# A vision tower on one core: the router's and the low-rank stage's first tiles moved among the attention values, with two reorderings of the attention scores

## Chip, cores and metric

The kernel runs on one core of one Trainium2 chip. The metric is the device time of one execution in microseconds (us). Before the change three runs gave 822.62, 823.07 and 823.40 us, median 823.07.

Names: TensorE is PE, its weight load PEld, VectorE DVE, ScalarE ACT, GpSimd POOL, SyncE SP.

## What is computed

A batch of 128 images goes through a patch tokenizer (9 window tokens and a class token per image, 256 channels), then two layers of attention and a mixture:

```
h = tokenizer(x)                                   # [128 images, 10 tokens, 256]
h = h + attention0(layernorm(h))                   # over the 10 tokens, 16 heads of 16 channels, two scores masked
h = h + experts(layernorm(h))                      # 8 experts, top 2 by router logits x @ router_w
h = h + attention1(layernorm(h))                   # causal, scores clipped to +-10
z = layernorm(h)                                   # low-rank stage
out = h + z @ base_W.T + base_b + shared(z) + sum_e gate_e(z) * (z @ A_e.T) @ B_e.T
                                                   # 6 experts of rank 16, top 2 of softmax(z @ router_W.T + b)
```

In both attentions each image attends over its own 10 tokens. All arithmetic is float32.

## The kernel before, in words

The 128 images are the partitions and a "tile" t (0 to 9, T = 10) is one token of all images: h is [128, 10 x 256]. Each engine's program is written out by hand in order, and semaphores alone join them, so an instruction queued behind a waiting one waits with it. `phase` (L280) is a barrier of all engines; one stands ahead of attention 0's softmax (1), one behind the experts (2), one ahead of the low-rank stage (3).

**Attention scores.** TensorE makes query, key and value of a tile (L1281), ScalarE copies them out (L1352). A score is an elementwise product of 256 channels, summed by 16. VectorE multiplies and sums some rows itself (L1448, L1454); GpSimd makes the other products (L1122, jobs in the order of `pool_jobs`) and VectorE sums them (L1460). In layer 0 two columns' products are summed by TensorE instead (L1250: 16 matmuls with the identity). In `pool_end` GpSimd does jobs 4 and 5, then waits for the last row's variance and raises it to -1/2 (`inverse_std`), then jobs 6 to 9.

**Softmax.** The ten rows are two halves, tiles 0 to 4 and 5 to 9. Layer 0 (L1502 to L1513): maximum and subtraction of half 0, of half 1 (VectorE), exp of each (ScalarE, L1400), `spread_values` (ScalarE, L1361), then for each half sum, reciprocal and two scalings (L1470). In layer 1 the exp is per row (L1372); half 0 is scaled after VectorE has summed row 7.

**Values** (L1301, L1222, L1514). For tiles 0, 2, 4, 6, 8 (layer 1: 0 to 4, 6, 8) GpSimd multiplies values by weights (L1155) and, over 5 keys, folds the upper half of the keys onto the lower (L1170); TensorE sums the keys by matmuls with the identity and so transposes (L1315). The other tiles are VectorE's: product (L1180), sum (L1521), a transposition on TensorE (L300). ScalarE copies the result (L1407), TensorE projects it and adds h (L1332, L1333), ScalarE writes h (L1366), VectorE takes its mean and variance (`add_o`, L1535). `add_o(4)` comes behind VectorE's tile 9 in its queue. TensorE's order is:

```
for t in range(T):
    turn_o(t)              # the sum of tile t
    if t: project_o(t - 1)
project_o(T - 1)
```

**Router** (L1587, L1693, L1788). Behind the values: ScalarE normalises the rows in groups of tiles 0 to 3, 4 to 7, 8 and 9 (`norm_rows`; group 0 at t = 7 of the values), TensorE transposes (L1593) over three banks, ScalarE copies (L1699), TensorE makes 8 logits a tile (L294), VectorE finds the top two (L1795 to L1801) and builds the routing tables. Then come 27 slots of experts (L1631, L1639).

**Low-rank stage** (L1947 to L2041), behind barrier 3: ScalarE normalises ten tiles, TensorE transposes over four banks and multiplies by `z_w`, 118 columns (two banks); VectorE copies them (L2011) and adds the base bias to h. Then VectorE adds the router bias, ScalarE takes one exp of all ten tiles (L1999), VectorE finds the top two and scales the low-rank vectors (L2033, L2034), while TensorE multiplies all tiles by `z_base` (L1969, 40 matmuls into five banks). Last, tile by tile, TensorE transposes z_s (L1976), ScalarE copies, TensorE multiplies by `z_b` (L1979), VectorE adds h for two tiles at a time (L2041), and SP stores them.

## Time and profile before

| | |
|---|---|
| median of three runs | 823.07 us |
| the profiled execution | 819.8 us, its span 817.7 us |
| TensorE busy | 88% of the span |
| DVE, POOL, ACT busy | 62%, 51%, 46% |
| mean granted TensorE clock | 0.941 of 2.4 GHz |
| attention 0, scores' end to last logits | 404 to 478 us |
| experts | 499 to 698 us |
| attention 1 and low-rank stage | 709 to 815 us |

Times in the trace count from the start of the span. Each timeline line gives the start, the duration, engine, source line, operation, output and inputs with their shapes, how many instructions are merged, and in brackets the idle time before it with the engine and line that ended it.

### The profile page before, as it was taken

The numbers are of one execution on the slowest core, as the hardware profiler recorded it, in microseconds if no ns is written. First come the engines' busy times: TensorE is split into PE (matmuls) and PEld (weight loads), VectorE is DVE, ScalarE is ACT, GpSimd is POOL, SyncE is SP. The second block draws the span as 40 slices with busy tenths as digits, with TensorE's granted clock in tenths as the row PEclk, the third lists the DMA queues.
The fourth block names the chain that finished last, engine by engine and source line by source line (L and its number), as shares of the span: only waits on it lengthen the run. The fifth ranks groups of instructions, "written<-read, shape, count | busy, mean of one in ns | idle before, by whom it ended". The sixth has DMA issues, their size and how long they took to land.

```text
span 817.7 us, 12959 instructions
## 1 busy us (share of the span) xinstructions
PE 716.3 (88%) x4311; PEld 616.5 (75%) x4311; DVE 508.0 (62%) x1233; ACT 374.7 (46%) x935; POOL 414.1 (51%) x279
## 2 busy tenths in 40 slices
PE   3979999999999999999808755999999999495978
PEld 3869998988989898655607645999999999353866
DVE  3668787778778677769799561222222222588956
ACT  3555565656556555533131422444444444165251
POOL 3755757677575761348849602433333432226820
PEclk9989999999999999999967956999999999699899
DMA  8642223212312120000020065889988881400001
GB/s 260 189 131 66 69 90 89 73 62 89 90 56 79 45 79 25 1 1 0 1 104 1 37 264 215 322 321 309 341 332 336 328 308 71 166 6 1 1 1 64
DMA packets 34487, 102.73 MB, mean 126 GB/s; under 512 B 3624, under 2 KB 12152, under 8 KB 27000
## 3 DMA queue, kind: packets, MB, share of 16 engines
q1 hardware_dynamic: 31832, 94.84, 33.5%
q0 software_dynamic: 2592, 7.10, 2.3%
q8 instruction: 35, 0.57, 0.3%
q14 instruction: 28, 0.23, 0.1%
HBM read 95.75 MB, written 6.17 MB: 125 GB/s over the span
## 4 chain that ended last, share of the span: by engine, by line
PE 73%; POOL 9%; DVE 9%; issue 2%; DMA 2%; ACT 2%; POOLq 1%; SPq 0%; DVEq 0%; ACTq 0%
PE banks L1631 12%; PE banks L1639 11%; PE banks L287 10%; PE banks L289 10%; PE banks L288 10%; PE banks L294 6%; PE banks L300 4%; POOL a_prod L1155 3%; PE banks L1285 2%; POOL a_prod L1170 2%; PE banks L1315 2%; POOLq L282 1%; PE banks L1969 1%; DVE banks L1438 1%; POOL rstd L336 1%
## 5 line engine op out<-in xcount | busy, mean ns | idle before, releaser
L401 POOL TENSOR_TENSOR x_lo<-xraw,x_hi 128x640 fp32r<-128x640 f32 x81 | 128.5, 1594 | 105.1 <-ACT x_hi L395 105.1
L287 PE MATMUL banks<-wc_hi,x_hi 128*128 128x256 f32 x405 | 120.6, 298 | 14.2 <-POOL x_lo L401 14.1
L1729 ACT ACTIVATE hid<-banks,b 128x128 f32<-128x128 f32 x216 | 79.3, 367 | 109.9 <-PE banks L1631 109.9
L288 PE MATMUL banks<-wc_lo,x_hi 128*128 128x256 f32 x405 | 115.7, 286 | 0.0
L289 PE MATMUL banks<-wc_hi,x_lo 128*128 128x256 f32 x405 | 115.6, 286 | 0.0
L287 PEld LDWEIGHTS banks<-wc_hi,x_hi 128*128 128x128 f32 x405 | 78.4, 194 | 16.3 <-issue 14.8
L1888 DVE TENSOR_TENSOR res<-banks,xb 128x256 f32<-128x256 f32 x27 | 11.5, 424 | 127.1 <-PE banks L1639 127.1
L288 PEld LDWEIGHTS banks<-wc_lo,x_hi 128*128 128x128 f32 x405 | 78.5, 194 | 1.8 <-issue 0.2
L424 DVE BATCH_NORM_STATS2 stats<-banks 128x6 f32<-128x256 f32 x81 | 34.7, 428 | 71.8 <-ACT pe_sb L418 71.1
L418 ACT ACTIVATE pe_sb<-banks 128x256 f32<-128x256 f32 x81 | 31.0, 383 | 105.4 <-PE banks L289 105.4
L289 PEld LDWEIGHTS banks<-wc_hi,x_lo 128*128 128x128 f32 x405 | 78.4, 194 | 0.0
L287 PE MATMUL banks<-wkv_hi,xg_hi 128*128 128x512 f32 x162 | 71.0, 438 | 6.4 <-DVE xg_lo L485 6.2
L1767 POOL TENSOR_TENSOR y<-bve,mhalf 128x1 f32<-128x1 f32 x27 | 20.2, 747 | 105.2 <-DVE bve L1896 105.2
L1631 PEld LDWEIGHTS banks<-xT,w_raw 128*128 128x128 f32 x448 | 67.7, 196 | 5.7 <-ACT xT L1717 0.9
L1631 PE MATMUL banks<-xT,w_raw 128*128 128x128 f32 x448 | 69.5, 280 | 0.5 <-ACT xT L1717 0.5
L1639 PE MATMUL banks<-w_raw,hid 128*128 128x256 f32 x224 | 66.9, 381 | 0.0
L1631 PEld LDWEIGHTS banks<-xT,w1more 128*128 128x128 f32 x416 | 61.9, 191 | 4.7
L289 PE MATMUL banks<-wkv_hi,xg_lo 128*128 128x512 f32 x162 | 64.5, 398 | 0.0
L288 PE MATMUL banks<-wkv_lo,xg_hi 128*128 128x512 f32 x162 | 64.0, 395 | 0.0
L1631 PE MATMUL banks<-xT,w1more 128*128 128x128 f32 x416 | 63.2, 275 | 0.0
L1285 PE MATMUL banks<-a_w,a_xT 128*128 128x512 f32 (+1 forms) x160 | 61.4, 519 | 0.4 <-DVE w_raw L1451 0.3
L1639 PE MATMUL banks<-w2more,hid 128*128 128x256 f32 x208 | 61.7, 381 | 0.0
(306 smaller groups left out, 1707.2 us busy)
## 6 DMA issues: line engine op xcount, KB each, us to landing
w_raw<-in_w SPq DMA_DIRECT2D x28, 1024.0 KB, 6.7
xraw<-in_x_main SPq DMA_DIRECT2D x27, 768.0 KB
w1more<-in_w SPq DMA_DIRECT2D x13, 1024.0 KB, 5.6
w2more<-in_w SPq DMA_DIRECT2D x13, 1024.0 KB, 8.2
xraw<-in_x_rest SPq DMA_DIRECT2D x27, 114.0 KB
yl<-y_rows SPq DMA_DIRECT2D x2, 1028.0 KB, 7.0
a_w<-in_qkv_w SPq DMA_DIRECT2D x2, 768.0 KB, 5.4
x_rows<-w_raw SPq DMA_DIRECT2D x5, 256.0 KB, 2.0
```

Of the source, the lines that this page charges most:

```text
L287: pe.matmul(dst, a[0], b[0], start=start, stop=False)
L288: pe.matmul(dst, a[0], b[1], start=False, stop=False)
L289: return pe.matmul(dst, a[1], b[0], start=False, stop=stop)
L294: last = pe.matmul(dst, aT[:, c * P:(c + 1) * P], w[:, c, a:b], start=(c == 0), stop=(c == CH - 1))
L300: last = pe.transpose(dst[:, c * P:(c + 1) * P], src[:, c * P:(c + 1) * P], ident[:, :])
L401: pool.tensor_tensor(x_lo[:, i % RING_X, :], xraw[:, k].rearrange("p c b -> p (c b)"), x_hi[:, i % RING_X, :], ALU.subtract).then_inc(sem( ...
L418: act.activation(pe_sb[:, i % RING_PE, :], bank(i % 2), ACT.Copy).then_inc(sem("pe_copied"), 1)
L424: dve.bn_stats(stats[0][:, k, :], bank(i % 2)).then_inc(sem("stats_made0"), 1)
L1285: last = pe.matmul(dst, a_xT[:, t % 2, c * P:(c + 1) * P], a_w[layer][:, c, a:b], start=(layer == 1 and c == 0), stop=(c == CH - 1))
L1631: last = pe.matmul(bank(fc % 2, 0, P), weights_of(s)[0][:, c * FF + fc * P:c * FF + (fc + 1) * P], xT[:, s % 2, c * P:(c + 1) * P], start= ...
L1639: last = pe.matmul(down_bank(s), hid[:, s % 2, fc, :], weights_of(s)[1][:, fc * C:(fc + 1) * C], start=(fc == 0), stop=(fc == FC - 1))
L1729: act.activation(hid[:, s % 2, fc, :], bank(fc % 2, 0, P), ACT.Gelu, bias=b1[:, bass.ds(e * FC + fc, 1)]).then_inc(sem("gelu_made"), 1)
```

## The change

Scores, layer 0: GpSimd does job 6 too ahead of its wait for the last row's variance. Softmax, layer 0: half 0 is summed and scaled ahead of the subtraction of half 1; ScalarE spreads the values after the first exp; half 1's softmax stands between VectorE's tiles 3 and 5. Maxima and sums go to PSUM bank 4. Layer 1: row 7's products are summed by TensorE, and half 0 is scaled after row 8. In both layers GpSimd's tile 8 is made in two halves of its keys, without a fold, and TensorE sums all its keys in two groups; `inverse_std` of the next stage's group 0 stands ahead of it. TensorE's and ScalarE's orders get the projection of tile 7 and then the next stage's tiles 0 to 3 (logits, or low-rank) in front of the sum of tile 8. Router: tiles 0 to 3 use one bank for transposing. Low-rank: barrier 3 is gone; `z_w` and base are one matrix of 374 columns, one bank for it and one for transposing; ScalarE copies out; the base bias is a row of `z_b`; GpSimd adds base and h; routing is done for tiles 0 to 7 and then 8 and 9; the buffers lie in `w_raw`. Declarations, the first lines of moved functions and the old low-rank code (see the kernel above) are left out here.

```diff
-        z_w = sb("z_w", [P, CH, ZW], F32, att)
-        z_b = sb("z_b", [LOW, C], F32, att)
-        z_base = sb("z_base", [P, CH, C], F32, att)
-        z_rows = sb("z_rows", [P, C + E6], F32, att)
+        z_w = sb("z_w", [P, CH, ZW + C], F32, att)
+        z_b = sb("z_b", [LOW + 1, C], F32, att)
+        z_rows = sb("z_rows", [P, E6], F32, att)
         tw = sb("tw", [P, T, 2], F32, att)
...
-                   ("low rank", 0, T - BT), ("low rank", T - BT, T)]
+                   ("low rank", 0, 4), ("low rank", 4, 8), ("low rank", 8, T)]
...
-            pool_scores(pool, 0, 4, 6)
+            pool_scores(pool, 0, 4, 7)
             inverse_std(pool, *batch_of("attention 0", 3))
-            pool_scores(pool, 0, 6, T)
+            pool_scores(pool, 0, 7, T)
...
+        ROW_ON_PE = T - 3
...
+            return (t, kind) in SUMS_ON_PE if layer == 0 else t == ROW_ON_PE
...
+        def in_two_parts(layer, t):
+            return layer in PARTED and t == POOL_VALUES[layer][-1]
...
+        PARTED = (0, 1)
+        def key_parts(layer, t):
+            n = kept_keys(layer, t)
+            return [(0, n // 2), (n // 2, n)] if in_two_parts(layer, t) else [(0, n)]
...
+                if t == POOL_VALUES[layer][-1]:
+                    inverse_std(pool, *batch_of(following, 0))
                 if folded(layer, t):
-                    pool_values(pool, layer, t).then_inc(sem("unfolded"), 1)
+                    pool_values(pool, layer, t, 0, keys(layer, t)).then_inc(sem("unfolded"), 1)
                     pool.wait_ge(sem("unfolded"), NW + 1 + made)
                     fold_pool_values(pool, layer, t).then_inc(sem("a_pool_values_made"), 1)
                 else:
-                    pool_values(pool, layer, t).then_inc(sem("a_pool_values_made"), 1)
-            if layer == 0:
-                for part in range(3):
-                    inverse_std(pool, *batch_of("experts", part))
-            else:
-                for part in range(2):
-                    inverse_std(pool, *batch_of("low rank", part))
+                    for a, b in key_parts(layer, t):
+                        pool_values(pool, layer, t, a, b).then_inc(sem("a_pool_values_made"), 1)
+            for part in range(1, 3):
+                inverse_std(pool, *batch_of(following, part))
+            if layer == 1:
+                pool_lora(pool)
...
+        def pe_sum_row(pe, t):
+            i = pool_jobs(1).index((t, "row", t + 1))
+            pe.wait_ge(sem("a_pool_prod_made"), len(pool_jobs(0)) + i + 1)
+            add_channels(pe, bank(6, 0, (t + 1) * H16), job_slot(1, i), t + 1)
...
+                for part, (a, b) in enumerate(key_parts(layer, t)):
+                    pe.wait_ge(sem("a_pool_values_made"), values_count(layer, t, part))
+                    for c in range(CH):
+                        for k in range(a, b):
+                            last = pe.matmul(bank(t % 2, c * P, (c + 1) * P), slot[:, k * C + c * P:k * C + (c + 1) * P],
+                                             ident[:, :], start=(k == 0 and c == 0), stop=(k == ns - 1 and c == CH - 1))
...
+                pe_sum_row(pe, ROW_ON_PE)
...
-                if t:
+                if t and t != T - 2:
                     project_o(t - 1)
+                if t == T - 3:
+                    project_o(t)
+                    if layer == 0:
+                        pe_logits(pe, 0)
+                    else:
+                        pe_lora(pe, 0)
             project_o(T - 1)
...
-                spread_values(act, 0, 0, T)
+                    if g == 0:
+                        spread_values(act, 0, 0, T)
...
-                if t:
+                if t and t != T - 2:
                     copy_h(act, layer, t - 1)
-                if layer == 0 and t == 7:
-                    norm_rows(act, 0)
+                if t == T - 3:
+                    copy_h(act, layer, t)
+                    if layer == 0:
+                        norm_rows(act, 0)
+                        for q in range(*GROUPS[0]):
+                            copy_x2T(act, q)
+                    else:
+                        act_lora(act, 0)
...
+            b = 6 if t == ROW_ON_PE else 4 if t == T - 1 else 7
...
+            if layer == 1 and t == ROW_ON_PE:
+                dve.wait_ge(sem("a_summed"), len(SUMS_ON_PE) + 1)
+                clip(dve, link, 1, "row", t, t + 1)
...
+            if layer == 0 and g == 0:
+                lower_half(dve, 1)
...
-                    if t == T - 1:
+                    if t == T - 2:
...
-                for g in range(2):
-                    s_g = half_scores(a_s, 0, g)
-                    max_g = a_max[:, g * HALF * H16:(g + 1) * HALF * H16].rearrange("p (t h) -> p t h", t=HALF)
-                    link(dve.tensor_reduce(max_g, s_g, AX, ALU.max))
-                    dve.tensor_tensor(s_g, s_g, max_g.unsqueeze(3).broadcast_to([P, HALF, H16, T]), ALU.subtract)\
-                       .then_inc(sem("a_s_made"), 1)
-                for g in range(2):
-                    softmax_half(dve, link, 0, g)
+                link(dve.tensor_reduce(top_bank(0), half_scores(a_s, 0, 0), AX, ALU.max))
+                lower_half(dve, 0)
+                link(dve.tensor_reduce(top_bank(1), half_scores(a_s, 0, 1), AX, ALU.max))
+                softmax_half(dve, link, 0, 0)
...
+                if layer == 0 and t == HALF:
+                    softmax_half(dve, link, 0, 1)
...
+                if layer == 0 and t == T - 3:
+                    route_top(dve, link, *GROUPS[0])
...
-            return ("experts", {3: 0, 7: 1, T - 1: 2}, 3) if layer == 0 else ("low rank", {7: 0, T - 1: 1}, 2)
+            return ("experts", {3: 0, 7: 1, T - 1: 2}, 3) if layer == 0 else ("low rank", {3: 0, 7: 1, T - 1: 2}, 3)
...
+            return bank(5) if t < GROUPS[0][1] else bank((2, 3, 0)[t % 3])
...
+        def turn_x2(pe, t):
+            pe.wait_ge(sem("x2_made"), t + 1)
+            if t:
+                pe.wait_ge(sem("x2T_made"), t if t < GROUPS[0][1] else max(t - 2, GROUPS[0][1]))
+            turn(pe, row_bank(t), x2[:, t * C:(t + 1) * C]).then_inc(sem("x2_turned"), 1)
+        def pe_logits(pe, g):
+            if g == 0:
+                pe.wait_ge(sem("moe_small_loaded"), 32)
+            a, b = GROUPS[g]
+            lead = 2 if g else 1
+            for t in range(a, a + lead):
+                turn_x2(pe, t)
+            for t in range(a, b):
+                if t + lead < b:
+                    turn_x2(pe, t + lead)
+                pe.wait_ge(sem("x2T_made"), t + 1)
+                mm_rows(pe, logits_at(t, t + 1), x2T[:, t % 4, :], w_rt, 0, E).then_inc(sem("lg_done"), 1)
...
+        def pe_lora(pe, g):
+            a, b = GROUPS[g]
+            if g == 0:
+                pe.wait_ge(sem("z_loaded"), 80)
             def turn_z(t):
                 pe.wait_ge(sem("z_xn_made"), t + 1)
+                if t:
+                    pe.wait_ge(sem("z_xT_made"), t)
+                turn(pe, bank(4), z_xn[:, t % 2, :]).then_inc(sem("z_turned"), 1)
+            turn_z(a)
+            for t in range(a, b):
                 pe.wait_ge(sem("z_xT_made"), t + 1)
+                if t + 1 < b:
+                    turn_z(t + 1)
+                if t:
+                    pe.wait_ge(sem("z_made"), t)
+                mm_rows(pe, bank(5, 0, ZW + C), z_xT[:, t % 2, :], z_w, 0, ZW + C).then_inc(sem("z_done"), 1)
+        def pe_lora_out(pe):
             for t in range(T + 1):
                 if t < T:
                     pe.wait_ge(sem("z_s_made"), 2 * (t + 1))
                     if t >= 2:
                         pe.wait_ge(sem("z_sT_made"), t - 1)
+                    pe.transpose(bank(t % 2, 0, P)[0:LOW + 1, :], z_s[:, t, :], ident[:, :]).then_inc(sem("z_s_turned"), 1)
                 if t:
                     pe.wait_ge(sem("z_sT_made"), t)
+                    if t >= T - 1:
+                        pe.wait_ge(sem("z_out_made"), 1)
+                    pe.matmul(out_bank(t - 1), z_sT[0:LOW + 1, (t - 1) % 2, :], z_b[:, :], start=(t % 2 == 1), stop=(t % 2 == 0))\
                       .then_inc(sem("z_out_done"), 1)
+        def act_lora(act, g):
+            a, b = GROUPS[g]
             def norm(t):
+                if t >= 2:
+                    act.wait_ge(sem("z_turned"), t - 1)
+                normalize(act, z_xn[:, t % 2, :], h_at(t), t, 1).then_inc(sem("z_xn_made"), 1)
+            def copy_z(t):
+                act.wait_ge(sem("z_done"), t + 1)
+                act.activation(z[:, t, :], bank(5, 0, ZW + C), ACT.Copy).then_inc(sem("z_made"), 1)
+            normalized_scales(act, "low rank", g)
+            norm(a)
+            norm(a + 1)
+            for t in range(a, b):
+                act.wait_ge(sem("z_turned"), t + 1)
+                if t >= 2:
+                    act.wait_ge(sem("z_done"), t - 1)
+                act.activation(z_xT[:, t % 2, :], bank(4), ACT.Copy).then_inc(sem("z_xT_made"), 1)
+                if t + 2 < b:
+                    norm(t + 2)
+                if t > a:
+                    copy_z(t - 1)
+            copy_z(b - 1)
+        ROUTED = [(0, 8), (8, T)]
+        def act_lora_out(act):
+            for i in range(2):
+                a, b = ROUTED[i]
+                act.wait_ge(sem("z_l_made"), i + 1)
+                act.activation(z_p[:, a:b, :], z_l[:, a:b, :], ACT.Exp).then_inc(sem("z_exp_made"), 1)
+                for t in range(a, b):
+                    act.wait_ge(sem("z_s_turned"), t + 1)
+                    if t >= 2:
+                        act.wait_ge(sem("z_out_done"), t - 1)
+                    act.activation(z_sT[0:LOW + 1, t % 2, :], bank(t % 2, 0, P)[0:LOW + 1, :], ACT.Copy).then_inc(sem("z_sT_made"), 1)
+        def pool_lora(pool):
             for t in range(T):
+                pool.wait_ge(sem("z_made"), t + 1)
+                pool.tensor_tensor(h_at(t), z[:, t, ZW:ZW + C], h_at(t), ALU.add).then_inc(sem("z_h_made"), 1)
+        def dve_lora(dve, link, i):
+            a, b = ROUTED[i]
+            n = b - a
+            cut = lambda x: x[:, a:b]
+            over = lambda x, m: cut(x).unsqueeze(2).broadcast_to([P, n, m])
+            if i == 0:
+                dve.wait_ge(sem("z_loaded"), 80)
+                dve.memset(z_s[:, :, LOW:LOW + 1], 1.0)
+                link(dve.memset(z_g[:, :, :], -1.0))
+            dve.wait_ge(sem("z_made"), b)
+            link(dve.tensor_tensor(cut(z_l), z[:, a:b, LOW:ZW], z_rows[:, :].unsqueeze(1).broadcast_to([P, n, E6]), ALU.add))
+            link(dve.tensor_reduce(cut(z_max), cut(z_l), AX, ALU.max))
+            dve.tensor_tensor(cut(z_l), cut(z_l), over(z_max, E6), ALU.subtract).then_inc(sem("z_l_made"), 1)
+            dve.wait_ge(sem("z_exp_made"), i + 1)
+            link(dve.tensor_reduce(cut(z_sum), cut(z_p), AX, ALU.add))
+            link(dve.reciprocal(cut(z_rec), cut(z_sum)))
+            link(dve.tensor_tensor(z_g[:, a:b, 0:E6], cut(z_p), over(z_rec, E6), ALU.mult))
+            top_two(dve, link, cut(z_g), cut(z_top), cut(z_topi), cut(z_topf), n)
+            link(dve.tensor_reduce(cut(z_sum), z_top[:, a:b, 0:2], AX, ALU.add))
+            link(dve.tensor_scalar(cut(z_sum), cut(z_sum), 1e-6, None, ALU.add))
+            link(dve.reciprocal(cut(z_rec), cut(z_sum)))
+            link(dve.tensor_tensor(cut(z_tw), z_top[:, a:b, 0:2], over(z_rec, 2), ALU.mult))
+            spread(dve, link, cut(z_topf), cut(z_tw), z_hot[:, :, a:b, :], cut(z_sw), E6, n)
+            for t in range(a, b):
                 dve.tensor_copy(z_s[:, t, 0:R16], z[:, t, 0:R16]).then_inc(sem("z_s_made"), 1)
                 dve.tensor_tensor(z_s[:, t, R16:LOW].rearrange("p (e r) -> p e r", e=E6),
                                   z[:, t, R16:LOW].rearrange("p (e r) -> p e r", e=E6),
                                   z_sw[:, t, :].unsqueeze(2).broadcast_to([P, E6, R16]), ALU.mult)\
                    .then_inc(sem("z_s_made"), 1)
+        def dve_lora_out(dve):
             for t in range(0, T, 2):
+                dve.wait_ge(sem("z_h_made"), t + 2)
                 dve.wait_ge(sem("z_out_done"), t + 2)
+                dve.tensor_tensor(h_at(t, 2), out_bank(t, 2), h_at(t, 2), ALU.add).then_inc(sem("z_out_made"), 1)
```

## Rows read from the trace of the kernel before

**Rows 1.** Page, part 4: shares of the chain that ended last.

```profile
PE 73%; POOL 9%; DVE 9%; issue 2%; DMA 2%; ACT 2%; POOLq 1%; SPq 0%; DVEq 0%; ACTq 0%
```

**Rows 2.** Timeline of VectorE: start, us, instruction [idle before <-releaser].

```profile
404.47 2.29 DVE L1438 TENSOR_REDUCE a_s<-a_prod 128x128 f32<-128x2048 f32 x1 [2.93 <-POOL a_prod L1122]
...
418.51 0.99 DVE L1510 TENSOR_TENSOR a_s<-a_s,a_max 128x800 f32<-128x800 f32 x1
...
425.18 2.82 DVE L1180 TENSOR_TENSOR a_prod<-a_prod,banks 128x2560 f32<-128x2560 f32 x1 [0.17 <-ACT a_prod L1361]
...
450.97 0.43 DVE L347 BATCH_NORM_STATS2 stats<-h 128x6 f32<-128x256 f32 x1 [1.52 <-ACT h L1366]
...
455.43 2.82 DVE L1521 TENSOR_REDUCE a_o<-a_prod 128x256 f32<-128x2560 f32 x1
...
477.69 0.17 DVE L1795 COPY lg<-banks 128x16 f32<-128x16 f32 x1 [0.43 <-PE banks L294]
```

**Rows 3.** Timeline of GpSimd, 365 to 480.

```profile
391.93 0.58 POOL L336 TENSOR_TENSOR rstd<-veps,mhalf 128x1 f32<-128x1 f32 x1 [3.17 <-DVE veps L354]
392.48 7.38 POOL L1122 TENSOR_TENSOR w_raw<-a_qkv 128x1536 f32<-128x1536 f32 x2
...
421.87 4.76 POOL L1155 TENSOR_TENSOR a_prod<-a_qkv,a_p 128x2560 f32<-128x2560 f32 x1 [5.02 <-DVE a_p L1487]
...
457.44 2.89 POOL L1170 TENSOR_TENSOR a_prod<-a_prod 128x1280 f32<-128x1280 f32 x1
```

**Rows 4.** Timeline of TensorE, 385 to 482.

```profile
399.32 11.56 PE L1259 MATMUL banks<-w_raw,ident 128*128 128x96 f32 x64
429.75 4.61 PE L1315 MATMUL banks<-ident,a_prod 128*128 128x128 f32 x20 [18.87 <-POOL a_prod L1170]
...
464.08 0.38 PE L300 MATMUL banks<-ident,a_o 128*128 128x128 f32 x2
```

**Rows 5.** Timeline of VectorE, attention 1.

```profile
751.92 2.29 DVE L1438 TENSOR_REDUCE banks<-w_raw 128x128 f32<-128x2048 f32 x1
...
776.26 2.82 DVE L1521 TENSOR_REDUCE a_o<-a_prod 128x256 f32<-128x2560 f32 x1
```

**Rows 6.** Timeline of TensorE, attention 1.

```profile
739.53 2.75 PE L1285 MATMUL banks<-a_w,a_xT 128*128 128x512 f32 x8
...
779.87 2.47 PE L1315 MATMUL banks<-ident,a_prod 128*128 128x128 f32 x20 [1.33 <-POOL a_prod L1170]
```

**Rows 7.** Timeline of ScalarE, the last copy of h.

```profile
786.48 0.38 ACT L1366 ACTIVATE h<-banks 128x256 f32<-128x256 f32 x1 [0.91 <-PE banks L1333]
```

**Rows 8.** Timeline of the low-rank stage, TensorE's base products and VectorE.

```profile
799.17 8.90 PE L1969 MATMUL banks<-z_base,z_xT 128*128 128x256 f32 x40 [0.38 <-DVE z L2011]
...
800.40 0.22 DVE L2021 TENSOR_REDUCE z_sum<-z_p 128x10 f32<-128x60 f32 x1 [0.32 <-ACT z_p L1999]
...
801.16 0.78 DVE L1548 MAX8 z_top<-z_g 128x8 f32<-128x8 f32 x10
...
806.10 0.17 DVE L2033 COPY z_s<-z 128x16 f32<-128x16 f32 x1
...
814.53 0.69 DVE L2041 TENSOR_TENSOR z_o<-banks,h 128x512 f32<-128x512 f32 x1 [0.49 <-PE banks L1979]
```

**Rows 9.** Groups of VectorE, 50 to 300: small tensor_scalars beside and without GpSimd.

```profile
L446 DVE TENSOR_SCALAR veps<-mv 128x4 f32<-128x4 f32 x7 | 6.5, 936 | 0.0
...
L448 DVE TENSOR_SCALAR veps<-mv 128x1 f32<-128x1 f32 x7 | 1.0, 142 | 0.0
```

**Rows 10.** Timeline of ScalarE, 415 to 482.

```profile
420.32 4.76 ACT L1361 ACTIVATE a_prod<-a_qkv 128x2560 f32<-128x2560 f32 x1
...
461.55 2.07 ACT L364 ACTIVATE w_raw<-h,nmr,rstd 128x256 f32<-128x256 f32 x4 [3.05 <-DVE nmr L341]
```

**Rows 11.** Windows: stretch, length, busy us (count) by engine, PEclk, DMA share, GB/s.

```profile
472.00:478.00 6.00, 5.59 (x32) 5.39 (x30) 2.59 (x29) 1.94 (x6) 0.00 (x0) 0.57 0.13 46
757.00:763.00 6.00, 5.74 (x18) 4.87 (x19) 5.21 (x6) 1.08 (x3) 4.77 (x4) 0.51 0.00 0
```

249 lines of the change are left out of this document (85 added, 164 removed).

## The prediction

> **What bounds the kernel now.** I read the page's shares of the chain that ended last first: TensorE carries 73% of it, GpSimd and VectorE 9% each [rows 1]. The conv rounds and the expert rounds, where TensorE carries the chain, are not touched by the change. So I went to the two attention tails and the low-rank stage, with the timelines of 385 to 480 us and of 698 to 818 us, engine by engine, and asked of each step which wait ended last.
>
> In attention 0 it is VectorE until the first softmax half is out: it idles 2.93 us for GpSimd's column product of tile 8 [rows 2], because GpSimd had itself sat 3.17 us waiting for the last row's variance [rows 3]. Then GpSimd's value products carry the chain: they start at 421.87, the last fold ends at 460.33, TensorE sums it and the router follows, whose last logits VectorE takes at 477.69 [rows 2, 3]. In attention 1 VectorE leads until the first half is scaled, then TensorE and GpSimd in turn; GpSimd's last fold ends at 779.73, TensorE sums it in 2.47 us from 779.87, VectorE's value 9 has been there since 779.08, and the last row of h is copied at 786.48 [rows 5, 6, 7]. From there the low-rank stage runs alone for 28.4 us: a barrier, ten tiles, VectorE's routing from 800.40, ten outputs; VectorE's last add ends at 815.22 [rows 8]. The store and the rest of the span end at 817.7.
>
> All times below are on the trace's clock. The profiled execution took 819.8 us, 3.3 less than the median 823.07; I add the change's microseconds to both. A measurement tells about 0.2% (1.6 us) from no change.
>
> **1. Column order.** The product of tile 6's column (3.4 of the 7.38 us for two [rows 3]) goes in front of GpSimd's wait and fills the 3.17 us idle. That alone would remove VectorE's 2.93 us. But VectorE's variance and centring instructions, which finished while GpSimd was idle, now meet a running GpSimd product. The trace shows what such a small tensor_scalar then costs: 936 ns (128x4) where the 128x1 form takes 142 [rows 9]. I take 0.75 us (the product's remaining 0.5 and then GpSimd's own wait behind the centring); ends 0 and 1.0. TensorE's channel sums (11.56 us for 64 matmuls from 399.32 [rows 4]) move 0.75 later with them, to 412.1 with their copy; VectorE needs them at 412.9, so they stay hidden with 0.8 to spare. Gain at the softmax: 2.93 - 0.75 = 2.2 us.
>
> The Trainium skill (SBUF — State Buffer, "Who interferes with whom") says that a tensor_scalar holds the port pair shared with GpSimd and that the second to issue fully blocks; by a mere slowdown of both the term would be near 2.9, by that rule it is the 2.2 above, and the two rows of [rows 9] agree with the rule.
>
> **2. Softmax order.** One subtraction (0.99 [rows 2]) leaves the way of half 0, so GpSimd starts 1.0 earlier, at 421.87 - 2.2 - 1.0 = 418.7. ScalarE's 4.76 us spread of the values [rows 10] no longer stands behind the second exp, so VectorE's values start at 421.2 instead of 425.18. The second half's softmax (four instructions, 2.8 us) now stands between VectorE's values 3 and 5; GpSimd needs it at 441.8 for tile 6 and has it at 435. VectorE's value 9 ends at 458.25 - 4.0 + 2.8 - 1.5 = 455.5, where the 1.5 is VectorE's idle before h(3), which the softmax now fills [rows 2]. The maxima and sums that now go to bank 4 instead of SBUF cost nothing: the lengths are the same and nothing waits for them twice (0 to 0.2).
>
> **3. Router rows among the values.** GpSimd's four products of 7.68 us (4.76 and 2.89 [rows 3]) end at 449.5; a power of about 1.1 (0.58 for one column [rows 3], here four) and two half products of 2.4 to 2.5 with no fold end at 455.8, 4.5 before the old end. But TensorE's queue now holds the logits of tiles 0 to 3 in front of the sum of tile 8. Their scales come from an instruction queued behind VectorE's value 9 and one tile's statistics: 456.1. ScalarE normalises four rows in 2.07 us [rows 10] to 458.3, then one bank makes transposition and copy alternate: 0.38 + 0.38 + two issues of 0.05 = 0.84 per tile [rows 4, 7], three times, and the last logits: 462.2. Only then do the 40 matmuls of tile 8 start, 0.11 each from 2.47 less its tail for 20 [rows 6]: 466.7, against 462.95 before. One projection (1.3, ScalarE's wait of 0.91 and 0.38 for a copy of h [rows 7]) is already done, so h(9) is ready at 470.4, against 467.45. Six tiles of logits remain instead of ten: 477.65 - 467.45 = 10.2 less 4 x 0.6 is 7.8, so 478.2. Net: **+0.5 us**. All that was won in 1 and 2 goes into this queue.
>
> **4. Attention 1 before the values.** TensorE sums row 7 instead of VectorE's 2.29 us [rows 5]: 32 matmuls at 0.18 to 0.20 [rows 4] from 747.8, done by about 754.1, when it idled before. The softmax of half 0 starts where that sum did, at 751.92, so GpSimd's values start 2.6 earlier; row 9's sum must wait for TensorE's and the clip and comes 1.9 earlier. ScalarE's last exp and TensorE's first projection come 1.9 earlier, and TensorE, which ran at half clock from 757 to 763 (granted 0.51 [rows 11]) after its queue had run dry, stays at 1.00. Projection 7 ends near 777.0; GpSimd's tile 8, in halves of four and five keys without a fold (0.48 a key [rows 3], so 1.9 and 2.4), ends at 776.8; VectorE's value 9 at 777.1 instead of 779.08.
>
> **5. Low-rank tiles 0 to 3 in front of tile 8.** Their scales again stand behind value 9: 777.5. First tile: 0.6 + 0.4 + 0.4, so its matmuls start at 779.5. They are four of 374 columns. Eight matmuls of mean 384 columns have a pitch of 2.59 (2.75 with the tail) [rows 6], 0.84 ns a column, so a tile takes 1.28, 1.46 until it can be read. It has one bank: ScalarE's copy (0.38 for 256 columns [rows 7], so 0.38 to 0.56 for 374; I take 0.5) must end before the next tile. Pitch: 1.46 + 0.5 + 2 x 0.05 = 2.05 to 2.1. TensorE is free for tile 8 at 779.5 + 3 x 2.08 + 1.3 = 787.0; its 36 matmuls take 4.1, transposition 9 with copy and two projections 3.7: h(9) at 794.9, against 786.86. **+8.0**, although GpSimd was 2.9 early.
>
> **6. The other six tiles.** 0.6 + 0.4 + 0.4 + 0.05 x 3 of lead-in, six pitches of 2.08 and a 1.4 bubble between the groups (the next group's normalising stands behind the last copy): tile 9 is copied at 810.7. Before, ten tiles were done at 799.1 and the 8.90 us of 40 base products ran beside the routing [rows 8]; now they are inside the pitch.
>
> **7. Routing and output.** The first exp stands in ScalarE's queue behind tile 9's copy, though tiles 0 to 7 were ready at 804.9. From z_sum (800.40) to the first scaled row (806.10) it took 5.7; less 2 x 0.23 for eight tiles instead of ten (0.08 for MAX8 [rows 8], twice that taken for the search) that is 5.2: from 810.95 to 816.2. Outputs go 0.59 a tile (two of them bring one add, 0.49 + 0.69 [rows 8]), eight of them: 820.9. Only then does ScalarE reach the second exp, and the second chain (5.7 less 8 x 0.23 less the shorter rows, 3.6) is serial: 824.9. Five adds of 0.69 [rows 8] behind it: 828.5. Against 815.2: **+13.3 us** for parts 4 to 7 together. GpSimd's ten new adds of 256 columns (0.5 to 0.75 each, a tenth of 4.76 [rows 3] and a start) mostly fall where VectorE waits: 0, or 1.4 if two stand in its way.
>
> **8. Clock.** TensorE idles from 810 to 816. After such gaps the granted clock was 0.51 (757 to 763) [rows 11], which is 1.2 GHz, and at 429.75 twenty matmuls took 4.61 [rows 4] instead of 2.47. Half clock makes an output tile about 1.1 instead of 0.59, for some four tiles: **+2.2** (0 to 4).
>
> The Trainium skill (TensorE: Matmul & The Clock Gate, "Part 1: The HAM clock gate") holds that an idle array falls to 1.2 GHz and regains 2.4 GHz only by sustained work; by that rule the 2.2 stands, without it the result is 837, and the clock rows agree.
>
> **Sum:** 0.5 + 13.3 + 2.2 = +16.0. From the median 839; the profiled execution 835.8.
>
> **Rivals.**
> (a) TensorE's clock also falls during the thin logits of part 3. For: from 472 to 478 the same small matmuls ran at 0.57 [rows 11]. Against: that was only the later part of ten tiles, here there are four. The 40 matmuls of tile 8 would take 9.1: +4.5, 843.5.
> (b) Output stays at full clock: 836.8.
> (c) The tiles slip in beside the values, the rest stands: if the scales came before projection 7 ended, h(9) would be at 785.2, 9.7 earlier: 829. Against: nothing lets the scales pass value 9.
> (d) Faster: TensorE alone paces the low-rank and router tiles, no shift or bank ever waits. It decides where tile 8's sum can start as GpSimd ends (776.8 and 455.8) and a tile costs 1.3, not 2.08: (c)'s -9.7, six tiles -4.7, early exp -3 with full clock -2.2, router -3.5 makes 23 less than my sum: about 816 to 819. For: TensorE idles now before tile 8's sum and again before the low-rank tiles. Against: the single bank and the queue order are in the code.
> (e) The overlap doesn't come about (the groups cost only what they cost at the end): about 823.
>
> **Chances.** Forecast 0.58, (a) 0.16, (b) 0.12, (c) 0.05, (d) 0.07, (e) 0.02. Faster 0.07, same 0.02, slower 0.91. The range 829 to 846 takes the forecast with its bounds (part 1's 1.0, the adds' 1.4, the clock's 0 to 4), (a), (b) and the edge of (c).
>
> **What would show it.** TensorE's sum of tile 8 starting near 787 with a wait on ScalarE's normalised or copied tile ahead of it, not on GpSimd; z tiles 2.1 us apart; h(9) near 795; the exp of the first group right behind the tenth copy; two routing chains with outputs between; the lg copy of the last group near 478. Wrong if the z tiles are under 1.6 us apart, or the sum of tile 8 starts within 1 us of GpSimd's end, or the last add comes before 820.

## The result: 20.7 us slower, and where the profile after puts it

The changed kernel took 843.58 us (median of four, 841.57 to 844.56) where the kernel before, measured beside it, took 822.85: ratio 1.0253, 95% interval 1.0232 to 1.0274. Its profiled execution took 844.56 us, 1.0 over its median; its span is 842.8 us, its mean granted clock 0.933 where before it was 0.941.

The page's shares of the chain that ended last, the line that answers to [rows 1]:

```profile
PE 76%; DVE 9%; POOL 7%; ACT 3%; DMA 2%; issue 2%; POOLq 1%; SPq 0%; DVEq 0%; ACTq 0%
```

TensorE carries 3% more, GpSimd 2% less: what was a wait for GpSimd's products has become TensorE's own queue. VectorE's timeline gives the landmarks (attention 0's last logits, attention 1's clip of row 8 and of row 7, the two chains of the low-rank router, the last add), to hold against [rows 2, 5, 8]:

```profile
392.13 0.53 DVE L1070 TENSOR_SCALAR agg<-h,mv 128x256 f32<-128x256 f32 x1
...
448.51 1.06 DVE L351 TENSOR_SCALAR veps<-mv 128x4 f32<-128x4 f32 x1
...
483.01 0.17 DVE L1936 COPY lg<-banks 128x16 f32<-128x16 f32 x1 [1.66 <-PE banks L291]
...
756.92 0.31 DVE L1478 TENSOR_SCALAR a_s<-banks 128x144 f32<-128x144 f32 x1
...
760.01 0.29 DVE L1478 TENSOR_SCALAR a_s<-banks 128x128 f32<-128x128 f32 x1 [0.86 <-PE banks L1282]
...
812.26 0.77 DVE L2098 TENSOR_TENSOR w_raw<-w_raw,z_rows 128x48 f32<-128x48 f32 x1 [7.81 <-ACT w_raw L2052]
...
818.22 0.20 DVE L2102 TENSOR_REDUCE w_raw<-w_raw 128x8 f32<-128x48 f32 x1 [4.71 <-ACT w_raw L2074]
...
831.00 0.17 DVE L2102 TENSOR_REDUCE w_raw<-w_raw 128x2 f32<-128x12 f32 x1 [5.31 <-ACT w_raw L2074]
...
838.15 0.69 DVE L2124 TENSOR_TENSOR h<-banks,h 128x512 f32<-128x512 f32 x1 [0.86 <-PE banks L2039]
```

The last logits come at 483.01 instead of 477.69, 5.3 later, though the masking that ends the scores came 2.3 earlier (412.97, before 415.31):

```profile
412.97 0.07 DVE L1560 MEMSET a_s<- 128x16 f32 x1 [0.26 <-DVEq L279]
```

and in the kernel before

```profile
415.31 0.07 DVE L1504 MEMSET a_s<- 128x16 f32 x1 [0.26 <-DVEq L282]
```

Up to attention 1 nothing changes (clip of row 8 at 756.92, before 751.58, again 5.3). From that clip to the end of the last add it then takes 81.9 us instead of 63.6: 18.3 more. So 5.3 + 18.3 = 23.6 us in these two executions, which lay 24.8 apart. That is 4 us more than the 20.7 between the medians: the profile before is of an execution 3 us under its median, this one is 1 us over.

TensorE's timeline: the end of the early logits, the sum of tile 8 (layer 0); the row sum moved to it, the early low-rank tiles, the sum of tile 8 (layer 1); the outputs. The rows before are [rows 4, 6, 8].

```profile
463.35 1.71 PE L291 MATMUL banks<-w_rt,w_raw 128*128 128x8 f32 x8
464.92 6.13 PE L1345 MATMUL banks<-ident,a_prod 128*128 128x128 f32 x40
...
752.84 7.14 PE L1282 MATMUL banks<-w_raw,ident 128*128 128x128 f32 x32
...
788.51 1.53 PE L291 MATMUL banks<-z_w,w_raw 128*128 128x374 f32 x4 [0.35 <-ACT w_raw L2052]
...
790.61 1.53 PE L291 MATMUL banks<-z_w,w_raw 128*128 128x374 f32 x4 [0.35 <-ACT w_raw L2052]
...
794.13 4.18 PE L1345 MATMUL banks<-ident,a_prod 128*128 128x128 f32 x36
...
823.54 0.80 PE L2034 MATMUL banks<-ident,w_raw 128*113 128x128 f32 x2 [6.01 <-DVE w_raw L2115]
824.47 1.22 PE L2039 MATMUL banks<-z_b,w_raw 113*128 113x256 f32 x2
```

Neither sum of tile 8 has a wait on GpSimd ahead of it any more: GpSimd was done at 455.6 and 783.7, and the sums start 9.3 and 10.4 us later, behind the early tiles. The early low-rank tiles stand 2.0 to 2.2 us apart (the two shown 2.10), each waiting 0.35 to 0.66 us behind ScalarE's copy (L2052). ScalarE's timeline shows the last copy of h [rows 7] and the two exponents:

```profile
801.68 0.38 ACT L1403 ACTIVATE h<-banks 128x256 f32<-128x256 f32 x1 [0.91 <-PE banks L1364]
...
817.57 0.48 ACT L2052 ACTIVATE w_raw<-banks 128x374 f32<-128x374 f32 x1 [1.68 <-PE banks L291]
817.95 0.24 ACT L2074 ACTIVATE w_raw<-w_raw 128x48 f32<-128x48 f32 x1
...
830.77 0.20 ACT L2074 ACTIVATE w_raw<-w_raw 128x12 f32<-128x12 f32 x1
```

Windows of the changed kernel (columns as in [rows 11]; the granted clock is the number behind POOL's):

```profile
461.00:465.00 4.00, 4.00 (x23) 3.94 (x21) 0.00 (x0) 1.15 (x3) 0.00 (x0) 0.51 0.17 66
465.00:468.00 3.00, 3.00 (x16) 3.00 (x16) 1.21 (x13) 0.00 (x0) 0.00 (x0) 0.52 0.00 0
468.00:472.00 4.00, 3.75 (x32) 3.48 (x31) 0.00 (x0) 0.66 (x2) 0.00 (x0) 1.00 0.02 4
...
820.00:824.00 4.00, 0.46 (x2) 0.46 (x2) 3.62 (x32) 0.00 (x0) 0.00 (x0) 0.50 0.00 0
824.00:828.00 4.00, 3.88 (x12) 2.98 (x12) 1.62 (x13) 1.08 (x4) 0.00 (x0) 0.50 0.00 0
```

The clock is at its lower level (1.2 GHz) during the early logits and half of the sum behind them, and again when the outputs begin.

### The profile page after: what moved, and what is told of

It reads as the page before. It is cut to its first block, busy times and chain, and to the rows that moved or that the text cites. A ratio compares the mean times of both kernels' runs of the same rounds, so it can differ in the third digit from the quotient of the medians.

```text
span 842.8 us, 13045 instructions
## 1 busy us (share of the span) xinstructions
PE 735.6 (87%) x4339; PEld 626.4 (74%) x4339; DVE 503.2 (60%) x1233; ACT 379.7 (45%) x946; POOL 416.4 (49%) x290
## 4 chain that ended last, share of the span: by engine, by line
PE 76%; DVE 9%; POOL 7%; ACT 3%; DMA 2%; issue 2%; POOLq 1%; SPq 0%; DVEq 0%; ACTq 0%
PE banks L1700 12%; PE banks L1708 11%; PE banks L284 10%; PE banks L286 10%; PE banks L285 10%; PE banks L291 7%; PE banks L297 4%; PE banks L1314 4%; PE banks L1345 3%; POOL a_prod L1153 2%; PE banks L1363 2%; DVE a_s L1483 2%; POOL a_prod L1182 1%; DVE h L1994 1%; PE banks L2039 1%
## 5 line engine op out<-in xcount | busy, mean ns | idle before, releaser
L421 DVE BATCH_NORM_STATS2 stats<-banks 128x6 f32<-128x256 f32 x81 | 34.7, 428 | 72.5 <-ACT pe_sb L415 71.7
L333 POOL TENSOR_TENSOR rstd<-veps,mhalf 128x5 f32<-128x5 f32 (+4 forms) x32 | 33.5, 1046 | 72.9 <-DVE veps L351 56.2
L1700 PE MATMUL banks<-xT,w1more 128*128 128x128 f32 x416 | 63.2, 274 | 0.0
```

The source lines that it names most:

```text
L333: pool.tensor_tensor(rstd[i][:, a:b], veps[i][:, a:b], mhalf[:, a:b], ALU.pow).then_inc(sem("rstd_made"), 1)
L421: dve.bn_stats(stats[0][:, k, :], bank(i % 2)).then_inc(sem("stats_made0"), 1)
L1700: last = pe.matmul(bank(fc % 2, 0, P), weights_of(s)[0][:, c * FF + fc * P:c * FF + (fc + 1) * P], xT[:, s % 2, c * P:(c + 1) * P], start= ...
```

## The experiments

Each kernel was timed in five rounds beside the kernel before. The table puts all on the landmarks of their traces (us): M the masking that ends attention 0's scores, L the last logits copy, C the clip of row 8 in attention 1, H the start of the last copy of h, E the end of the last add. M itself wanders by 2 us between kernels that are the same up to it, so the differences L-M and E-C are what to compare; they wander too, by 1.5 to 1.7 us between kernels with the same code there (E-C of the changed kernel and of c3, L-M of the seven kernels with the early router rows).

| kernel | ratio (95%) | M | L | C | H | E | L-M | E-C |
|---|---|---|---|---|---|---|---|---|
| before | 1 | 415.31 | 477.69 | 751.58 | 786.48 | 815.22 | 62.4 | 63.6 |
| changed | 1.0253 (1.0232 to 1.0274) | 412.97 | 483.01 | 756.92 | 801.68 | 838.84 | 70.0 | 81.9 |
| c1_column_order | 0.9979 (0.9969 to 0.9988) | 412.88 | 478.73 | 752.03 | 786.87 | 815.56 | 65.9 | 63.5 |
| c2_without_moved_tiles | 0.9950 (0.9933 to 0.9968) | 412.70 | 475.36 | 749.05 | 783.22 | 812.45 | 62.7 | 63.4 |
| c3_router_behind | 1.0174 (1.0157 to 1.0190) | 414.03 | 476.39 | 751.13 | 795.87 | 831.56 | 62.4 | 80.4 |
| c4_lowrank_behind | 1.0283 (1.0268 to 1.0299) | 414.93 | 483.64 | 756.99 | 791.69 | 837.81 | 68.7 | 80.8 |
| c5_two_banks | 1.0195 (1.0170 to 1.0221) | 412.88 | 481.28 | 754.99 | 797.59 | 830.70 | 68.4 | 75.7 |
| c6_first_exponent_early | 1.0212 (1.0184 to 1.0240) | 412.67 | 481.08 | 755.18 | 799.94 | 833.33 | 68.4 | 78.2 |
| c7_both_exponents_early | 1.0155 (1.0129 to 1.0181) | 413.88 | 483.93 | 757.84 | 802.60 | 831.10 | 70.1 | 73.3 |
| c8_fillers | 1.0278 (1.0253 to 1.0304) | 414.75 | 483.45 | 756.90 | 801.61 | 839.03 | 68.7 | 82.1 |
| e1_narrow_product | 1.0158 (1.0140 to 1.0176) | 414.24 | 482.90 | 756.11 | 797.28 | 830.95 | 68.7 | 74.8 |
| e2_all_repaired | 1.0015 (0.9999 to 1.0030) | 414.15 | 476.46 | 751.00 | 792.70 | 817.48 | 62.3 | 66.5 |
| e3_fold_kept | 0.9971 (0.9957 to 0.9985) | 413.18 | 474.75 | 748.66 | 782.62 | 811.84 | 61.6 | 63.2 |
| e4_fillers_in_router | 0.9924 (0.9899 to 0.9950) | 412.91 | 473.15 | 746.43 | 780.37 | 809.60 | 60.2 | 63.2 |

### Which part of the change costs

**c1: the column order alone.**

```diff
-            pool_scores(pool, 0, 4, 6)
+            pool_scores(pool, 0, 4, 7)
...
-            pool_scores(pool, 0, 6, T)
+            pool_scores(pool, 0, 7, T)
```

> The kernel before with the column order of the tail alone (GpSimd makes job 6 in its first call and jobs 7 to 9 in its second). By the forecast's first step the softmax starts 2.2 us earlier and nothing behind it moves: ratio 0.9973 (0.9965 to 0.9985), 820.6 us. Rival: GpSimd's transfer of work does not delay VectorE's small operations, then -2.9 us, 0.9965. Rival: the gain is hidden by the values' own order, then 1.000. In the trace of the changed kernel the memset ahead of the softmax came 2.3 us earlier, so the first is the likelier.

Measured 820.27 us, -1.7 (-2.5 to -1.0). From the variance (L354) to the masking it took 20.9 us instead of 23.6: 2.7 are won. In this profile the router gave it all back (L-M 65.9 instead of 62.4): the granted clock was 0.50 from 470 to 478, before 0.67. By the times it is a gain, inside the range expected and a little under the size forecast.

**c2: all but the moved tiles.** The router and the low-rank stage are those of before, the rest is the change's. TensorE's order against the changed kernel's; ScalarE's order and the old router and low-rank code, put back likewise, are left out.

```diff
             for t in range(T):
                 turn_o(t)
-                if t and t != T - 2:
+                if t:
                     project_o(t - 1)
-                if t == T - 3:
-                    project_o(t)
-                    if layer == 0:
-                        pe_logits(pe, 0)
-                    else:
-                        pe_lora(pe, 0)
             project_o(T - 1)
```

> The kernel before with every part of the change but the moved tiles: column order, softmax order, tile 8 of GpSimd's values in two parts that TensorE sums whole, row 7 of attention 1 summed on TensorE; router and low-rank stage stay behind the last tile. If the parts beside the moved tiles are gains and the whole loss lies in the moved tiles and in the cut-up low-rank stage: last logits copy of layer 0 some 5 us earlier than before (column and softmax order 3.2, no fold of tile 8 1.7 to 2), attention 1 another 2 us earlier, in all 815 us (812 to 818), ratio 0.991. Rival: the tile-8 sum of all keys on TensorE at half clock takes back what the fold saved: 819 to 821, 0.997. Rival: the softmax and values parts themselves lose: over 823.

Measured 817.54, -4.1 us: faster than the kernel before, so the whole loss lies in the moved tiles and the new low-rank stage; but half the gain expected, nearer the first rival. TensorE and GpSimd around tile 8 of layer 0:

```profile
449.24 4.88 POOL L1156 TENSOR_TENSOR a_prod<-a_qkv,a_p 128x1280 f32<-128x1280 f32 x2
```

```profile
449.42 3.73 PE L1347 MATMUL banks<-ident,a_prod 128*128 128x128 f32 x20 [2.40 <-POOL a_prod L1185]
...
456.18 4.63 PE L1347 MATMUL banks<-ident,a_prod 128*128 128x128 f32 x40
```

GpSimd has tile 8 ready at 454.1. TensorE, with no idle from 449.4 on, comes to it at 456.2 and takes 4.63 us for 40 products where the folded tile took 2.47 for 20. It ends at 460.8, 48.1 after the masking; before it was 47.6. The softmax order's gain and the fold's removal end there. Part of this is the clock: the sum of tile 6 took 3.73 us (granted 0.67 from 449 to 453) and the projection behind it 1.45, where the same rows took 2.47 and 1.03 in c3, 1.7 us less together.

**c3: the router's early rows back behind the values.**

```diff
                     project_o(t)
-                    if layer == 0:
-                        pe_logits(pe, 0)
-                    else:
+                    if layer == 1:
                         pe_lora(pe, 0)
...
                         norm_rows(act, 0)
-                        for q in range(*GROUPS[0]):
-                            copy_x2T(act, q)
```

> The changed kernel with router tiles 0 to 3 behind the values as before (normalized rows still made early; banks and order of the router as before). In the changed kernel the clock fell to 0.51 among those rows' thin matmuls and the tile-8 sum behind them took 6.1 us instead of 4. Theory (the early rows hold the last tiles back): the tile-8 sum starts at about 461 to 462 and ends at 466, and the router then needs its 12 us behind it: -2 to -6 us, 839 us (ratio to the changed kernel 0.995, to the kernel before about 1.020). Rival: the early rows were worth what they cost: within 1 us of 843.6 (1.025). Rival: they gained, the kernel is 2 to 4 us slower than the changed one (1.029).

The router's old order, with three banks for transposing, comes back with it; that part of the edit is left out above.

Measured 835.96, ratio 1.0174: 0.8% below the changed kernel's, 6.5 us, just over the end of the range expected. L-M falls from 70.0 to 62.4, exactly the old length. The sum of tile 8:

```profile
457.15 4.63 PE L1345 MATMUL banks<-ident,a_prod 128*128 128x128 f32 x40
```

7.8 us earlier (8.8 counted from M) and 1.5 shorter than the changed kernel's. But 1.7 us of the 8.8 are not the edit's: ahead of both sums the two kernels have the same instructions, and there the sum of tile 6 ran at the lower clock in the changed kernel's execution alone (see step 3 below). The early rows cost more in front of tile 8 than they save behind it.

**c4: low-rank tiles 0 to 3 behind the last projection.**

```diff
-                    else:
-                        pe_lora(pe, 0)
             project_o(T - 1)
+            if layer == 1:
+                pe_lora(pe, 0)
```

> The changed kernel with low-rank tiles 0 to 3 behind the last projection, otherwise the new pipelined form. Theory (what costs is the form: one bank for z, the exponent behind tile 9's copy, the clock of the output phase; the place of four tiles matters little, since the chain of ten tiles is as long either way): 842.5 to 845, ratio 1.025. The forecast's fifth step prices the place at +8.0 for the last h copy and gives four tiles less behind it, 4 x 2.1 = 8.4: -0.4. Rival: the insertion itself loses because tile 8's and 9's sums wait and nothing is saved: 836 to 839. Rival: it gains as meant, then this kernel is at 850 (1.034).

H comes 10.1 us earlier after C (34.7 us instead of 44.8), and E-C is 80.8 instead of 81.9: what four tiles cost in front of tile 8 they cost behind it. The place is worth little either way, as expected; the ratio, 0.3% above the changed kernel's with intervals that overlap, and the trace, 1.1 us below, leave the sign open.

### What in the new low-rank stage costs

**c5: two banks for the product.**

```diff
-                if t:
-                    pe.wait_ge(sem("z_made"), t)
-                mm_rows(pe, bank(5, 0, ZW + C), z_xT[:, t % 2, :], z_w, 0, ZW + C).then_inc(sem("z_done"), 1)
+                if t >= 2:
+                    pe.wait_ge(sem("z_made"), t - 1)
+                mm_rows(pe, bank((5, 2)[t % 2], 0, ZW + C), z_xT[:, t % 2, :], z_w, 0, ZW + C).then_inc(sem("z_done"), 1)
...
-                act.activation(z[:, t, :], bank(5, 0, ZW + C), ACT.Copy).then_inc(sem("z_made"), 1)
+                act.activation(z[:, t, :], bank((5, 2)[t % 2], 0, ZW + C), ACT.Copy).then_inc(sem("z_made"), 1)
```

> The changed kernel with two PSUM banks in turn for the low-rank product instead of one, so that TensorE's next tile need not wait for ScalarE's copy. Theory (the tile pitch of 2.1 us is product 1.42 + copy 0.48 + hand-over): the product no longer waits for the 0.48 us copy; TensorE then needs 0.38 for the transposes and 1.3 to 1.42 for the product: pitch 1.6 to 1.75, seven tiles gain 0.4 each (those that do not stand behind a normalization): -2.5 to -3.5 us, ratio to before 1.0215. Rival: the transposed rows' one bank holds the pitch at 2.1: 0, 1.0255. Rival: ScalarE is late with the normalizations: -1.

E-C 75.7, 6.2 less; by the ratios 4.8. More than expected, since the pitch is 1.48 and not 1.6 to 1.75: the product holds TensorE for 1.26 us before the next transposition starts, and that for 0.22 before the next product, less than the durations of both rows:

```profile
799.77 1.43 PE L291 MATMUL banks<-z_w,w_raw 128*128 128x374 f32 x4
801.03 0.38 PE L297 MATMUL banks<-ident,w_raw 128*128 128x128 f32 x2
801.25 1.43 PE L291 MATMUL banks<-z_w,w_raw 128*128 128x374 f32 x4
```

1.48 us from tile to tile, TensorE never idle: the single bank was 0.62 of the 2.10.

**c6 and c7: the exponents.** c6 moves the first one up in ScalarE's queue (the first added lines; the second exponent stays between the copies of tiles 7 and 8); c7 moves the second also (the last added line), with the three VectorE operations that it needs.

```diff
                 act.activation(z_xT[:, t % 2, :], bank(4), ACT.Copy).then_inc(sem("z_xT_made"), 1)
+                if t == 8:
+                    act_exponent(act, 0)
...
         def act_lora_out(act):
+            act_exponent(act, 1)
             for i in range(2):
```

> The changed kernel with the first exponent of the low-rank router (tiles 0 to 7) moved in ScalarE's queue from behind the copy of tile 9 to behind the transposed copy of tile 8. Theory (forecast step 7: the exponent behind tile 9's copy holds the first chain back): it runs at 813.6 to 814 instead of 817.95, the first scaled row comes at 819.1 instead of 823.5, all behind it moves along: -4.4 us, ratio to before 1.020. Rival: the first chain was covered, what ends the kernel is TensorE at half clock: -1 or less, 1.0245. Rival: tile 8's and 9's copies come later by the exponent: 0.

> As the last kernel, and the second exponent (tiles 8 and 9) ahead of the copies of the output phase, with its three VectorE operations ahead of the row scalings. Theory: the second chain no longer waits for the outputs (VectorE idle 5.3 us in the changed kernel) and hides behind them: -4.4 and another 2 to 3, then the ten outputs at 1.06 us each at half clock are the bound: -6 to -7.5 us in all, ratio to before 1.017. Rival: the rows of group one are held up by the three operations and the copy of tile 9: -4 to -5, no better than the last kernel.

c6: E-C 78.2, -3.8; c7: 73.3, -8.7 (by the ratios -3.4 and -8.1). The first is a little less than expected, the two together a little more. In c7 ScalarE, and VectorE's second chain:

```profile
814.46 0.24 ACT L2075 ACTIVATE w_raw<-w_raw 128x48 f32<-128x48 f32 x1
...
820.73 0.21 ACT L2075 ACTIVATE w_raw<-w_raw 128x12 f32<-128x12 f32 x1 [1.75 <-DVE w_raw L2101]
```

```profile
822.58 0.15 DVE L2116 TENSOR_REDUCE w_raw<-w_raw 128x2 f32<-128x12 f32 x1
```

The wait of 5.31 us ahead of the second chain is gone, and the chain runs beside the outputs. The place of two instructions of 0.2 us in a queue (for the second, with the three VectorE operations it needs) was worth 8 us, nearly half of the low-rank loss.

**c8: added products ahead of the outputs.**

```diff
         def pe_lora_out(pe):
+            pe.wait_ge(sem("z_xT_made"), T)
+            for k in range(15):
+                pe.matmul(bank(4, 0, ZW + C), ident[:, :], z_w[:, k % CH, :], start=True, stop=True)
```

> The changed kernel with 15 added products of 0.355 us each on TensorE (a free bank, read by nobody) between the last low-rank product and the outputs, where it is idle for 6 us and the granted clock falls from 1.0 to 0.50. Theory (step 8, the clock of the output phase): the six outputs that came at a pitch of 1.06 us come at 0.54: -3 us, and with them the second exponent; ratio to before 1.0215. Rival: the clock falls all the same: 0. Rival: the added products last into the outputs and push them: +1 or more.

```profile
817.29 9.60 PE L2031 MATMUL banks<-z_w,ident 128*128 128x374 f32 x30
826.73 0.38 PE L2037 MATMUL banks<-ident,w_raw 128*113 128x128 f32 x2
```

```profile
824.00:832.00 8.00, 7.34 (x32) 4.91 (x30) 1.97 (x15) 2.21 (x9) 0.00 (x0) 1.00 0.00 0
```

The second rival, in part: one product is two of the trace's matmuls and costs 0.64 us, not the 0.355 that I had taken for it, so the fifteen last 9.6 us and the outputs begin 3.2 late. But the clock stayed at 1.00, and the outputs of tiles 0 to 7, 0.55 to 0.64 us apart, ended only 0.5 later than the changed kernel's (the last at 830.92, there 830.39). So the lower clock cost the output phase 2.7 us in the changed kernel's trace. E-C is 82.1 against 81.9, and the ratio, 1.0278, is 2 us higher with intervals that overlap: the kernel as a whole shows no gain.

**e1: the product 118 columns wide, as before the change.**

```diff
-                mm_rows(pe, bank(5, 0, ZW + C), z_xT[:, t % 2, :], z_w, 0, ZW + C).then_inc(sem("z_done"), 1)
+                mm_rows(pe, bank(5, 0, ZW), z_xT[:, t % 2, :], z_w, 0, ZW).then_inc(sem("z_done"), 1)
...
-                act.activation(z[:, t, :], bank(5, 0, ZW + C), ACT.Copy).then_inc(sem("z_made"), 1)
+                act.activation(z[:, t, 0:ZW], bank(5, 0, ZW), ACT.Copy).then_inc(sem("z_made"), 1)
...
-                pool.tensor_tensor(h_at(t), z[:, t, ZW:ZW + C], h_at(t), ALU.add).then_inc(sem("z_h_made"), 1)
+                pool.tensor_tensor(h_at(t), h_at(t), h_at(t), ALU.add).then_inc(sem("z_h_made"), 1)
```

> The changed kernel with the low-rank product 118 columns wide, as before the change, instead of 374. It leaves out the constant product (GpSimd's additions run at their size but add the tile to itself). Theory: what made a tile cost 2.1 us is that the 256 constant columns now stand on the path of every tile; in the kernel before they ran behind the last tile, 8.9 us of TensorE under VectorE's chain. Product 0.60 instead of 1.42, copy 0.28 to 0.36 instead of 0.48: pitch about 1.15, seven tiles by 0.95 and the rest less: -7 to -9 us, ratio to before 1.016. Rival: with one bank and four hand-overs a tile the width matters little: -3, 1.021. Rival: thin products drop the clock, then the tile-8 sum and the last projections pay it back: -4, 1.020.

```profile
787.00 0.70 PE L291 MATMUL banks<-z_w,w_raw 128*128 128x118 f32 x4
...
788.06 0.70 PE L291 MATMUL banks<-z_w,w_raw 128*128 128x118 f32 x4
```

1.06 us apart, E-C 74.8, -7.1, ratio 1.0158 (-7.8): the theory's size, although from 800.7 the thinner products ran at the lower clock (up to 1.21 us each), as the last rival had it. In the kernel before the constant's 8.90 us of TensorE ran under VectorE's routing [rows 8]; folding it into the product put it on the path.

**e2: all repairs at once** (c3, c5, c7 and four added products).

> The changed kernel with all repairs at once: router tiles behind the values, two banks for the low-rank product, both exponents early, four short added products on TensorE ahead of the outputs. Theory (the losses are separate and add up): -6.6 (router) -4.8 (banks) -8.1 (exponents) -1 to -2 (clock) from 843.6 gives 822 to 824, ratio to before 1.000 (0.997 to 1.004): the moved low-rank stage is then worth no more than the old place. Rival: the exponents and banks overlap in what they free: 828, 1.008. Rival: with the repairs the early tiles pay: below 0.993.

823.18 us, ratio 1.0015: the kernel before. The repairs add up (c3 -6.5, c5 -4.8, c7 -8.1 are 19.4 together; e2 has 19.6, with the clock's share), so the losses are separate and these are all but 2.8 us of E-C. And the new low-rank stage, repaired, wins nothing: c2, which differs in having the old one, has 0.9950, 5.3 us less, and 63.4 instead of 66.5 for E-C.

### A kernel that beats both

**e3: c2 with GpSimd's fold of tile 8 kept.**

```diff
-        PARTED = (0, 1)
+        PARTED = ()
```

> The kernel without the moved tiles, and with tile 8 of GpSimd's values folded by GpSimd as before in both layers, so that TensorE sums 20 (layer 0) products of it instead of 40. In the kernel without the moved tiles TensorE had no idle time from tile 7's sum to the last projection of layer 0, and GpSimd was done 2 us before the sum began. Theory (TensorE is the bound there, the fold was the cheaper way): tile 8's sum of layer 0 ends 1.3 us earlier, of layer 1 0.5 to 0.8 earlier: 815.5 us, ratio to before 0.9928 (the kernel without the moved tiles had 0.995). Rival: GpSimd, 2.9 us later, is the bound again: same or +1, 0.995 to 0.996.

```profile
457.57 2.47 PE L1347 MATMUL banks<-ident,a_prod 128*128 128x128 f32 x20 [2.40 <-POOL a_prod L1185]
```

The sum of tile 8 in layer 0: in the trace it ends at 460.04, 46.9 after the masking (c2 48.1), L-M is 1.1 less and E-C 0.2 less. The times do not confirm it: 819.28, ratio 0.9971, and c2's was 0.9950 with an overlapping interval, measured in another set of runs. The expected 0.9928 is outside: with GpSimd's longer work the sum waits for it again (2.40), so the rival is nearer. The trace's 1.2 us up to the sum's end are not the fold's either: c2 lost 1.7 at the lower clock there, and e3's sum of tile 6 took 2.47. Without that loss c2's would end earlier than e3's (48.1 less 1.7 is 46.4, an estimate from these rows). Whether the fold pays stays open.

**e4: e3 and three added products in the router.**

```diff
                 mm_rows(pe, logits_at(t, t + 1), x2T[:, t % 4, :], w_rt, 0, E).then_inc(sem("lg_done"), 1)
+                if t == 0:
+                    for k in range(3):
+                        pe.matmul(bank(7), ident[:, :], x2[:, 0:C], start=True, stop=True)
```

> The last kernel (no moved tiles, folds kept) with three added products of 256 columns on TensorE (a free bank, read by nobody) in the 1.3 us in which it waits for ScalarE behind the first logits. In the trace without them the granted clock falls from 1.0 to 0.5 at about 469.7 us, in the middle of the thin logits, and the last four rows take 1.2 us each instead of 0.62. Theory (the added products keep the clock up as they did ahead of the outputs): the fall comes after the last logits, -2 us: ratio to before 0.9945 and the last logits copy at 472.7. Rival: the fall is put off by less than a microsecond or not at all: 0.9971, copy at 474.7. Rival: the added products last longer than the gap and push the logits: +0.5.

The windows 468 to 470 and 470 to 472 us of e3:

```profile
468.00:470.00 2.00, 2.00 (x21) 1.90 (x20) 0.93 (x11) 1.96 (x6) 0.00 (x0) 0.98 0.17 64
470.00:472.00 2.00, 2.00 (x11) 2.00 (x12) 0.28 (x5) 0.66 (x2) 0.00 (x0) 0.50 0.37 139
```

and the added products and the same windows of e4:

```profile
465.11 1.54 PE L1648 MATMUL banks<-w_raw,ident 128*128 128x256 f32 x6
```

```profile
468.00:470.00 2.00, 2.00 (x20) 1.89 (x20) 1.19 (x13) 2.00 (x6) 0.00 (x0) 1.00 0.05 18
470.00:472.00 2.00, 2.00 (x17) 2.00 (x17) 0.55 (x6) 0.78 (x3) 0.00 (x0) 0.79 0.38 134
```

The added products fill the wait exactly (465.11 to 466.65). The clock falls 1.2 us later (471.15 instead of 469.9; 1.5 later counted from M), TensorE gets 37 matmuls done in these 4 us instead of 32, and the last logits copy comes at 473.15, L-M 1.3 less than e3's. 815.24 us, ratio 0.9924 (0.9899 to 0.9950): the fastest kernel here, 6.4 us under the kernel before it was timed with. The 3.9 us by which the ratios of e3 and e4 differ are more than the trace's 1.3 (spans 814.3 and 812.7); they come from different sets of runs, and what the rest is stays open.

## Why the prediction held, step by step

The direction and its reason were right: the moved tiles and the new low-rank stage eat what the reorderings win. 839 was forecast, 843.6 came. By the traces part 3 (with 1 and 2) came out 4.8 us worse than forecast and parts 4 to 8 together 2.8; that is more than the 4.7 by which the medians exceed the forecast, for the profiled executions lie further apart than the medians. The larger share is part 3's, where rival (a) came about.

**1. Column order.** Forecast -2.2, measured -2.3 at M, or -2.7 if counted from the variance (c1). VectorE's centring beside GpSimd's product took 0.53 us, before 0.34: the lock that I priced at 0.75 cost 0.2 here, within the bounds given. The port lock itself is in the trace elsewhere: the variance of 128x4 at 448.51 took 1.06 us and ended with GpSimd's fold (446.66, 2.88 us), where the same form took 0.17 at 459.04 with GpSimd idle, so the 936 ns of [rows 9] are the lock and not the form. And the 48-column addition at 812.26 took 0.77, started 0.02 behind GpSimd's addition (812.24, 0.72 us), where one of the same size took 0.21 at 813.30. By the Trainium skill (SBUF — State Buffer, "Who interferes with whom") the second to issue can be blocked fully, a tensor_scalar in a mode that takes both ports, or an operation with two inputs in SBUF beside a GpSimd one that reads SBUF; these two rows agree.

**2. Softmax order.** GpSimd's values start at 418.78 (418.7 forecast), VectorE's value 9 ends at 455.14 (455.5), GpSimd is done at 455.6 (455.8).

**3. Router rows: this step failed in size.** "Net: +0.5" was +5.3 in the trace, since the granted clock fell to its lower level, where the sum had all of this at full clock. It fell at 461, with the second transposed row. So a row took 1.22 us instead of 0.84, and the sum of tile 8 began at 464.92 (462.2 forecast) and took 6.13 (4.5), half of it at the lower clock: 471.05 instead of 466.7. The rest is as forecast: 8.2 us from h(9) to the last logits (7.8).

Most of the late start arose ahead of the rows. The forecast lets ScalarE normalise them when their scales are there, at 456.1. The scales were there at 455.74, but ScalarE's new order has the copy of h(7) in front:

```profile
455.61 0.13 DVE L338 SCALAR_TENSOR_TENSOR nmr<-mv,rstd 128x4 f32<-128x4 f32 x1
```

```profile
457.95 0.38 ACT L1403 ACTIVATE h<-banks 128x256 f32<-128x256 f32 x1 [0.91 <-PE banks L1364]
458.23 2.06 ACT L361 ACTIVATE w_raw<-h,nmr,rstd 128x256 f32<-128x256 f32 x4
```

Of these 2.1 us, 1.7 are TensorE's clock again. The sum of tile 6, with the projection behind it (1.63 us here, 1.03 in c3), in the changed kernel and in c3, whose instructions up to there are the same:

```profile
449.69 3.56 PE L1345 MATMUL banks<-ident,a_prod 128*128 128x128 f32 x20 [2.40 <-POOL a_prod L1182]
```

```profile
450.74 2.47 PE L1345 MATMUL banks<-ident,a_prod 128*128 128x128 f32 x20 [2.39 <-POOL a_prod L1182]
```

In nine traces with the same code up to there ScalarE starts 45.3 us after M in two (the changed kernel and c7) and 43.6 in the others: whether the sum of tile 6 meets the lower clock is a matter of the single execution, and so is that part of the +5.3.

Rival (a) had the mechanism and, with +4.5, the size, though it put the loss in the sum alone: 1.6 of the 4.4 us by which the sum ends late are in the sum, the rest ahead of it. Its argument against itself, that four tiles are too few, was wrong. c3 prices the rows at 6.5 us. No run held the clock up under them, so how these divide between the clock and the place in the queue is not shown.

**4. Attention 1.** Row 7's sum took 7.14 us (6.3 forecast), so VectorE waited 0.86 for it, and TensorE did not stay at full clock: its first projection at 764.37 took 1.63 instead of 1.03. Counted from C, value 9 ended 0.7 earlier than before, not 2.0. c2 shows that the row's gain does not reach the end (E-C 63.4 against 63.6): its last copy of h comes 0.7 us earlier after C than before, and the low-rank stage behind it takes 0.5 longer. The unfolded tile 8 costs TensorE 4.18 where the folded cost 2.47, but e3, which folds it, gains only 0.2 more.

**5. Low-rank tiles.** The pitch was 2.10 (2.05 to 2.1 forecast). H came 9.9 later than before, counted from C (+8.0 forecast); 1.3 of that is part 4's. c5 and e1 show the pitch's parts: the single bank 0.62, the 256 constant columns 1.04.

**6, 7. Six tiles and the two chains.** From the end of h(9)'s copy to the end of tile 9's copy 16.0 us (15.8 forecast; its terms add up to 15.4); from there to the end 20.8 (20.0 with part 8). c6 and c7 confirm both waits: the first exponent behind tile 9's copy 3.8, the second between the outputs' copies another 4.9.

**8. Clock of the outputs.** The forecast had four tiles at about 1.1; there were five, each 1.0 to 1.2 us behind the last, and c8 puts it at 2.7 (+2.2 forecast; four tiles at 1.1 instead of 0.59 make 2.0). In the other traces with these outputs two to five are that far apart, so 2.7 is near the upper end.

In all parts 4 to 8 were forecast at +15.5 and came to +18.3. Rival (d), that the tiles cost only TensorE's own time and make the kernel faster (816 to 819), is what e2 tests: with these waits repaired the changed kernel gives 823.2, still no gain. In layer 0 that is no surprise, since its router is back in the old place; in the low-rank stage TensorE is the bound either way, before with the constant's products beside the routing, afterwards with them inside the tiles.

## What to carry to other kernels

Work moved into an engine's idle time must be ready before that time: here its scales came from the last step of the engine beside it, so the four tiles stood in front of the work that all waited for, and cost there what they saved behind. When a stage is cut up to be pipelined, look at what the old form hid for nothing (a wide product under another engine's chain), how many banks each hand-over has, and where single small instructions stand in their queue: two exponents of 0.2 us were worth 8 us. And time the parts of a bundle one by one: all but the moved tiles were worth 4 us here, the moved tiles with the new low-rank stage lost 25.

## What the runs showed of the hardware that I had not expected

TensorE's clock fell while TensorE was busy. In e3 its last wait, of 1.34 us, ended at 467.12; from there to 472 it is busy without a gap, and the granted clock falls at 469.9 (0.98 from 468 to 470, 0.50 from 470 to 472, busy 2.00 of 2.00 us in both). In the changed kernel it fell at 461, right behind two waits of 1.05 and 1.33 us, and stayed at 0.51 through 461 to 465, busy 4.00 of 4.00 us with nothing but transpositions and products of 8 columns. From 468 on, in the sum of 40 products of 128 columns that came behind them without a gap, it was back at 1.00. The same instructions can meet either level: the sum of tile 6 took 3.56 us in the changed kernel's execution and 2.47 in c3's. And it can be held up: products that nobody reads kept it at 1.00 through the outputs (c8) and put its fall off by 1.2 us in the router (e4), where they cost nothing because they filled a wait. The Trainium skill (TensorE: Matmul & The Clock Gate, "Part 1: The HAM clock gate") ties the lower clock to an idle array; here rows show it under a busy one as well.

M wandered by 2 us (412.67 to 414.93) between kernels whose instructions are the same up to it, and the layer-0 part L-M between 68.4 and 70.1 among seven kernels with the same code there. E-C was 81.9 and 80.4 in the changed kernel and c3, which have the same code behind C. A single trace's landmark or stretch is no better than that, so small steps were read as differences inside one stage.
